# Keys times values straight from SBUF, values centred by their weight, and two projections side by side, in a three-stage transformer block

## The chip, the cores and the metric

The kernel runs on one core of a Trainium2 chip. The metric is the device time of one execution in microseconds (us); of several runs the median is given. PE is TensorE, DVE VectorE, ACT ScalarE, POOL GpSimd, SP the engine that only issues DMAs.

## The reference, cut to what matters

The input is `x` of 2 x 1024 tokens with 128 channels. Three stages follow each other:

```
x = x + 0.5 * ffn(layernorm(x))      # 8 experts, 128 -> 512 -> 128, the best 2 of 8 count
x = x + attn(layernorm(x))
x = x + 0.5 * ffn(layernorm(x))
```

Every expert is computed for every token and weighted by its gate. `attn` is a linear recurrence with 4 heads of 16 keys and 32 values:

```
r, k, v, g = four projections of token-shifted mixtures of x
w = tanh((x + delta * w_mu) @ A_w.T) @ B_w.T + b_w
S_t = exp(-exp(w_t)) * S_{t-1} + k_t v_t^T
o_t = r_t . (S_{t-1} + u * k_t v_t^T)
o = (o - mean(o)) / sqrt(var(o) + eps)        # over the 32 values of each head
attn = (o * gn_weight + gn_bias) * silu(g) @ W_o.T
```

`mean(o)` is linear in `v`, since `o` is.

## The kernel before, in words

**Layout.** The channels lie on the 128 partitions and 512 tokens are one tile, so there are 4 tiles (2 sequences, 2 halves each), and 8 blocks of feed-forward work (4 tiles before the attention, 4 after). The second halves take the recurrence's state over from the first.

**The slots.** The program is written out by hand as 256 slots `n`, one for each block, expert and quarter of the hidden width (`SLOTS`, `ALL`). In each slot PE computes one quarter up (`ffn_up`, L353, three matmuls L363, L364, L367 in fp32r, a split of fp32 into an upper and a lower part) and one quarter down, three slots late (`ffn_down`, L369). The quarter down is one fp32 matmul (L397), or, where `in_parts(n)` says so, three fp32r matmuls (L388, L390, L393), for which ACT writes `hid_hi` (L596) and DVE subtracts `hid_lo` (L798). ACT makes the relu of each quarter (L595, L598). After the four quarters of an expert DVE weights them with the gates (`combine`, L807) and POOL adds them to `x` (`add_y`, L954).

**The attention units.** Between the slots' feed-forward work stand the steps of the attention, one unit `i` for each tile (0 and 1 are the first halves, 2 and 3 the second). `UNIT` gives the slot where a unit begins, `step_of` its step `t` in slot `n`, and each engine's program has a function `attend(i, t)` that says what it does in that step. Every engine works strictly in the order written.

- `T_PR` (t = 12 to 14): projections. PE multiplies `u` by `A_w` (L502, bank A2, rows 0 to 63) and `W_r` (L503, bank A2, rows 64 to 127), by `W_k` (L506, all 128 rows of bank A1, the 64 outputs twice), and one slot on by `W_v` (L510); the last three through `proj`, whose matmul is L461. ACT takes the tanh (L652), copies `q` twice (L654, L655), `kk` (L657) and `v` (L660) out of PSUM. DVE forms `quk = q * bonus * kk` (L878).
- SP writes `v` to DRAM and reads it back as `vb`, one of 16 groups of rows at a time, each value row repeated over its keys (`values`, L289, `fetch`, L608). `vb` has 5 buffers.
- `T_SC` (t = 18 to 37): the recurrence, 16 steps `m` in 20 slots (`scan_at`). For each, ACT copies `vb` into one of three PSUM banks (`show`, L624), DVE multiplies that bank in place by `kk` (`keys_times_values`, L840; one step ahead), scans it along time with `dec` into a state buffer `S` (L856), and POOL multiplies the state by `q` (`read_state`, L995) after it has saved or seeded the carry (L992 or L1001, 1 column). There are 4 state buffers and 8 buffers `qs`.
- `REDUCE` (t = 25, 30, 35, 39): PE sums 4 of the `qs` over the keys (L469). `ROUTE` and other numbers place the router's small steps.
- `T_PO` (t = 40): PE centres `o` by a matmul (L523), ACT squares it (L672), DVE scales it (L894), and the variance, the output projection and the addition to `x` follow up to t = 48.

Of the kernel before, what the change touches and what calls it, by code (L numbers as in the profile page):

```python
# [5 lines left out]
ALU = mybir.AluOpType  # L6
# [146 lines left out]
def program(nc, xT_in, xtok_in, wexp_in, small_in, const_in, gate_dram, v_dram, out):  # L153
    with ExitStack() as ctx:
        def sb(name, shape, dt=F32):
            return ctx.enter_context(nc.sbuf_tensor(name, shape, dt))
# [87 lines left out]
        xa_zero, xa_prev, xm_r, z_p, z_r, mus, mterm, u_r = (sem(n) for n in ("xa_zero", "xa_prev", "xm_r", "z_p", "z_r", "mus", "mterm", "u_r"))  # L244
        pr, aw_r, q_r, k_r, quk_r, bet, bet_c, bv_r = (sem(n) for n in ("proj", "aw_r", "q_r", "k_r", "quk_r", "beta", "beta_c", "bv_r"))
        v_r, sg_t, sg_r, wb_r, e_r, dec_r = (sem(n) for n in ("v_r", "sg_t", "sg_r", "wb_r", "e_r", "dec_r"))
        vp, kv_r, st_r, qs_r, red, o_r, seed, s_zero = (sem(n) for n in ("vp", "kv_r", "st_r", "qs_r", "red", "o_r", "seed", "s_zero"))
        cen, sq_r, var_p, ysc_r, yoff_r, yo_r, yp, x_att = (sem(n) for n in ("cen", "sq_r", "var_p", "ysc_r", "yoff_r", "yo_r", "yp", "x_att"))

# [4 lines left out]
        def _(sp):  # L254
# [34 lines left out]
            def values(i):  # L289
                sp.wait_ge(v_r, i + 1)  # L290
                for d in range(VD):
                    sp.dma_start(v_dram[i].rearrange("(r d) n -> r d n", d=VD)[:, d, :], v[:, :]).then_inc(v_out[i], 16)
                sp.wait_ge(v_out[i], 16 * VD)
                for m in range(VS):
                    n = i * VG + m
                    if n >= VS:
                        sp.wait_ge(vp, n - VS + 1)
                    sp.dma_start(vb[:, n % VS, :], value_rows(v_dram[i], m)).then_inc(v_in[n % VS], 16)
# [51 lines left out]
        def _(pe):  # L350
# [95 lines left out]
            def mus_of(i, n):  # L446
                if n == 0:
                    pe.wait_ge(z_r, 2 * i + 1)
                if n == 2:
                    pe.wait_ge(z_r, 2 * i + 2)  # L450
                if n >= 3:
                    pe.wait_ge(mterm, 5 * i + n - 2)
                dst, c = A[MUS_BANK[n]][:, :], MIX[n]
                if c < 4:
                    mm(dst, w(W_X2, P, slice(32 * c, 32 * c + 32)), z0[32 * c:32 * c + 32, :],
                       start=True, stop=True).then_inc(mus, 1)
                else:
                    mm(dst, w(W_X2B, P, slice(0, 32)), z1, start=True, stop=True).then_inc(mus, 1)
# [14 lines left out]
            def attend(i, t):  # L473
# [25 lines left out]
                if t == T_PR:  # L499
                    pe.wait_ge(mterm, 5 * i + 4)  # L500
                    pe.wait_ge(u_r, 5 * i + 2)
                    mm(A[2][0:64, :], w(W_A, 64), u[:, 1, :], start=True, stop=True).then_inc(pr, 1)  # L502
                    mm(A[2][64:P, :], w(W_R, 64), u[:, 0, :], start=True, stop=True).then_inc(pr, 1)  # L503
                    pe.wait_ge(mterm, 5 * i + 5)
                    pe.wait_ge(u_r, 5 * i + 3)
                    proj(i, 1, W_K, 2)  # L506
                if t == T_PR + 1:
                    pe.wait_ge(q_r, i + 1)
                    pe.wait_ge(u_r, 5 * i + 4)
                    proj(i, 2, W_V, 3)  # L510
                    pe.wait_ge(aw_r, i + 1)
                    pe.wait_ge(quk_r, i + 1)
                    mm(A[0][:, :], w(W_B, P, slice(0, 64)), aw[0:64, :], start=True, stop=True).then_inc(wb_r, 1)
                    mm(A[1][:, :], const[64:P, C_BET:C_BET + P], quk[64:P, :], start=True, stop=True).then_inc(bet, 1)
# [4 lines left out]
                if t in REDUCE:  # L519
                    reduce(i, REDUCE.index(t))  # L520
                if t == T_PO:
                    pe.wait_ge(o_r, i + 1)
                    mm(A[0][:, :], const[:, C_CEN:C_CEN + P], o[:, :], start=True, stop=True).then_inc(cen, 1)  # L523
                if t == T_VAR:
# [35 lines left out]
        def _(act):  # L560
# [47 lines left out]
            def fetch(i, m):  # L608
                n = i * VG + m
                act.wait_ge(vp, n - VS + 1)  # L610
                act.dma_start(vb[:, n % VS, :], value_rows(v_dram[i], m)).then_inc(v_in[n % VS], 16)

            def show(i, m):
                n = i * VG + m
                if m == 0:
                    act.wait_ge(bet_c, i + 1)
                if m == 1:
                    act.wait_ge(bv_r, i + 1)
                if m == 2:
                    act.wait_ge(sg_r, i + 1)  # L620
                if m >= 3:
                    act.wait_ge(st_r, n - 2)
                act.wait_ge(v_in[n % VS], 16 * (n // VS + 1))
                act.activation(A[STATE_BANK[m % 3]][:, :], vb[:, n % VS, :], ACT.Copy).then_inc(vp, 1)  # L624

            def attend(i, t):
                h, b = home(i)
                if t == T_NRM:
                    normalise(LN_ATT[i], A[0])
                if scan_at(t + 1) == 0:  # L630
                    show(i, 0)
                if scan_at(t + 1) is not None and scan_at(t + 1) + 1 < VG:
                    m = scan_at(t + 1) + 1
                    show(i, m)
                    if m + VS - 1 < VG:
                        fetch(i, m + VS - 1)
                if t == T_CHN:
# [12 lines left out]
                if t == T_PR:  # L650
                    act.wait_ge(pr, 5 * i + 1)
                    act.activation(aw[0:64, :], A[2][0:64, :], ACT.Tanh).then_inc(aw_r, 1)  # L652
                    act.wait_ge(pr, 5 * i + 2)
                    act.activation(q[0:64, :], A[2][64:P, :], ACT.Copy)  # L654
                    act.activation(q[64:P, :], A[2][64:P, :], ACT.Copy).then_inc(q_r, 1)  # L655
                    act.wait_ge(pr, 5 * i + 3)
                    act.activation(kk[:, :], A[1][:, :], ACT.Copy).then_inc(k_r, 1)  # L657
                if t == T_PR + 1:
# [11 lines left out]
                if t == T_PO:  # L670
                    act.wait_ge(cen, i + 1)
                    act.activation(sq, A[0][:, :], ACT.Square).then_inc(sq_r, 1)  # L672
                    act.activation(y_off, sg[:, :], ACT.Identity, scale=w(W_GB, 1)).then_inc(yoff_r, 1)
# [23 lines left out]
        def _(dve):  # L697
# [138 lines left out]
            def keys_times_values(i, m):  # L836
                n = i * VG + m
                bank = A[STATE_BANK[m % 3]][:, :]
                dve.wait_ge(vp, n + 1)
                dve.tensor_tensor(bank, bank, kk[:, :], ALU.mult).then_inc(kv_r, 1)  # L840

            def scan(i, m):
                n, (h, b) = i * VG + m, home(i)
                bank = A[STATE_BANK[m % 3]][:, :]
                if m == 0:
                    keys_times_values(i, 0)
                if m + 1 < VG:
# [11 lines left out]
            def attend(i, t):  # L859
# [15 lines left out]
                if t == T_PR:  # L875
                    dve.wait_ge(q_r, i + 1)
                    dve.wait_ge(k_r, i + 1)
                    dve.scalar_tensor_tensor(out=quk[:, :], in0=q[:, :], scalar=w(W_U, 1), in1=kk[:, :],  # L878
                                             op0=ALU.mult, op1=ALU.mult).then_inc(quk_r, 1)
# [12 lines left out]
                if t == T_PO:  # L892
                    dve.wait_ge(sq_r, i + 1)
                    dve.scalar_tensor_tensor(out=y_sc, in0=A[0][:, :], scalar=w(W_GW, 1), in1=sg[:, :],  # L894
                                             op0=ALU.mult, op1=ALU.mult).then_inc(ysc_r, 1)
# [175 lines left out]
def lay_out(d):  # L1071
# [62 lines left out]
```

## Time and profile before

| | |
|---|---|
| median of 3 runs | 481.19 us (480.6 to 481.32) |
| the profiled execution's own time | 481.31 us |
| its span, first to last instruction | 479.5 us |
| PE busy | 466.3 us, 97% |
| DVE busy | 389.5 us, 81% |
| ACT busy | 341.2 us, 71% |
| POOL busy | 250.8 us, 52% |
| granted TensorE clock | 0.999 of full speed |
| chain that ended last | PE 61%, DVE 16%, issue 11%, POOL 5%, ACT 4%, DMA 2% |

Times in the views count from the first instruction. Matmuls are pipelined, so a PE row's length holds the time behind its neighbours too; the pace of PE is read from one start to the next.

### The profile page before, as it was taken

How to read it: one execution, taken by the hardware profiler on the slowest of the kernel's cores; microseconds unless marked ns; L12 is line 12 of the kernel's file. 1: busy time of each engine (PE TensorE's matmuls, PEld its weight loads, DVE VectorE, ACT ScalarE, POOL GpSimd, SP SyncE). 2: the span in 40 equal slices, each digit the busy share in tenths (PEclk: the TensorE clock that was granted, in tenths of full speed). 3: DMA queues.
4: the chain of work that ended last, by engine and by line, in shares of the span. 5: the costliest groups of instructions: out<-in, count | busy, mean ns of one | idle time of the engine just before them, and what ended most of it. 6: DMA issues, size and time to landing. Idle time of an engine off the chain costs nothing.

```text
span 479.5 us, 6566 instructions
## 1 busy us (share of the span) xinstructions
PE 466.3 (97%) x1977; PEld 295.9 (62%) x1977; DVE 389.5 (81%) x714; ACT 341.2 (71%) x585; POOL 250.8 (52%) x266
## 2 busy tenths in 40 slices
PE   7999989999999999999999999999999999999996
PEld 3667656565556647555654756566565555777785
DVE  3889987869977896997696799967679994786986
ACT  3787767687758768774867777656878665688784
POOL 1658463627885172886516268834617874321322
PEclk9999999999999999999999999999999999999999
DMA  8761040157310018630003554121056501004200
GB/s 260 226 243 42 1 130 27 46 162 234 131 45 0 3 45 223 194 110 1 2 1 131 154 179 153 44 67 44 0 157 204 173 24 39 2 0 132 68 1 22
DMA packets 21298, 44.60 MB, mean 93 GB/s; under 512 B 3856, under 2 KB 4240, under 8 KB 21264
## 3 DMA queue, kind: packets, MB, share of 16 engines
q1 hardware_dynamic: 14928, 32.66, 21.6%
q10 hardware_dynamic: 6336, 11.54, 8.1%
q8 instruction: 16, 0.26, 0.2%
q14 instruction: 18, 0.15, 0.1%
HBM read 40.91 MB, written 3.28 MB: 92 GB/s over the span
## 4 chain that ended last, share of the span: by engine, by line
PE 61%; DVE 16%; issue 11%; POOL 5%; ACT 4%; DMA 2%; POOLq 0%; SPq 0%; ACTq 0%; DVEq 0%
PE Y L397 13%; PE U L363 9%; PE U L367 8%; PE U L364 8%; DVE hid_lo L798 4%; PE Y L388 4%; PE Y L393 4%; PE Y L390 4%; PE A L469 3%; POOL xT L954 2%; DVE gy L807 2%; POOL qs L995 2%; PE A L461 1%; ACT hid_hi L596 1%; DMA G<-gate_dram 1%
## 5 line engine op out<-in xcount | busy, mean ns | idle before, releaser
L954 POOL TENSOR_TENSOR xT<-xT,gy 128x512 f32<-128x512 f32 x63 | 83.6, 1326 | 138.1 <-DVE gy L807 138.0
L363 PE MATMUL U<-xhi,w1lo 128*128 128x512 f32 x256 | 146.0, 570 | 1.9 <-ACT hid_hi L596 1.7
L798 DVE TENSOR_TENSOR hid_lo<-hid,hid_hi 128x512 fp32r<-128x512 f32 x140 | 117.1, 847 | 27.2 <-ACT hid_hi L596 25.8
L595 ACT ACTIVATE hid<-U,small 128x512 f32<-128x512 f32 x128 | 88.2, 689 | 41.9 <-PE U L367 37.6
L598 ACT ACTIVATE hid<-U,small 128x512 f32<-128x512 f32 x128 | 87.8, 689 | 41.6 <-PE U L367 38.9
L397 PE MATMUL Y<-hid,w 128*128 128x512 f32 x228 | 115.9, 589 | 0.0
L364 PE MATMUL U<-xhi,w1hi 128*128 128x512 f32 x256 | 100.8, 394 | 0.0
L367 PE MATMUL U<-xlo,w1hi 128*128 128x512 f32 x256 | 100.6, 393 | 0.0
L995 POOL TENSOR_TENSOR qs<-q,pool_a 128x512 f32<-128x512 f32 x64 | 79.9, 1248 | 16.0 <-DVE pool_a L856 16.0
L596 ACT ACTIVATE hid_hi<-U,small 128x512 fp32r<-128x512 f32 x128 | 87.6, 685 | 0.0
L363 PEld LDWEIGHTS U<-xhi,w1lo 128*128 128x128 f32 x256 | 48.1, 188 | 59.4 <-issue 33.3
L364 PEld LDWEIGHTS U<-xhi,w1hi 128*128 128x128 f32 x256 | 48.3, 189 | 27.5 <-issue 23.5
L367 PEld LDWEIGHTS U<-xlo,w1hi 128*128 128x128 f32 x256 | 48.0, 188 | 11.4 <-DVE xlo L734 0.4
L393 PE MATMUL Y<-hid_lo,w2hi 128*128 128x512 f32 (+1 forms) x134 | 52.5, 392 | 0.6 <-DVE hid_lo L798 0.6
L388 PE MATMUL Y<-hid_hi,w2lo 128*128 128x512 f32 (+1 forms) x134 | 52.1, 389 | 0.7 <-DVE hid_lo L798 0.7
L390 PE MATMUL Y<-hid_hi,w2hi 128*128 128x512 f32 (+1 forms) x134 | 52.0, 388 | 0.0
L624 ACT ACTIVATE A<-vb 128x512 f32<-128x512 f32 x64 | 38.1, 600 | 19.3 <-DVE pool_a L856 19.2
L807 DVE SCALAR_TENSOR_TENSOR gy<-Y,small,G 128x512 f32<-128x512 f32 x61 | 44.9, 736 | 5.1 <-DMA G<-gate_dram 3.6
L397 PEld LDWEIGHTS Y<-hid,w 128*128 128x128 f32 x228 | 42.8, 188 | 9.7
L840 DVE TENSOR_TENSOR A<-A,kk 128x512 f32<-128x512 f32 x64 | 43.1, 678 | 0.0
L856 DVE TENSOR_TENSOR_SCAN pool_a<-dec,carry,A 128x512 f32<-128x512 f32 x32 | 40.5, 1265 | 0.0
L856 DVE TENSOR_TENSOR_SCAN pool_a<-dec,A 128x512 f32<-128x512 f32 x32 | 38.5, 1204 | 0.0
(135 smaller groups left out, 526.6 us busy)
## 6 DMA issues: line engine op xcount, KB each, us to landing
G<-gate_dram SPq DMA_DIRECT2D x32, 512.0 KB, 4.5
vb<-v_dram ACTq DMA_DIRECT2D x44, 256.0 KB, 3.7
vb<-v_dram SPq DMA_DIRECT2D x20, 256.0 KB, 4.3
pool_a<-wexp_dram SPq DMA_DIRECT2D x8, 256.0 KB, 6.7
w<-wexp_dram SPq DMA_DIRECT2D x8, 256.0 KB, 6.6
v_dram<-v SPq DMA_DIRECT2D x8, 256.0 KB, 2.2
xnt<-xtok_dram SPq DMA_DIRECT2D x4, 256.0 KB, 4.9
xT<-xT_dram SPq DMA_DIRECT2D x4, 256.0 KB, 7.3
```

The costliest lines, as they stand in the source:

```text
L363: mm(dst, w1lo[:, e, f, :], xhi[:, k % NB, :], start=True, stop=False)
L364: mm(dst, w1hi[:, e, f, :], xhi[:, k % NB, :], start=False, stop=False)
L367: mm(dst, w1hi[:, e, f, :], xlo[:, k % NB, :], start=False, stop=True).then_inc(up, 1)
L393: last = mm(dst, w2hi[:, g % E, f, :], hid_lo[:, at, cut], start=False, stop=final)
L397: last = mm(dst, w2[:, g % E, f, :], hid[:, n % HS, cut], start=first, stop=final)
L595: act.activation(hid[:, n % HS, :], U[n % 2][:, :], ACT.Relu, bias=bias)
L596: act.activation(hid_hi[:, c % PS, :], U[n % 2][:, :], ACT.Relu, bias=bias).then_inc(h_f, 1)
L598: act.activation(hid[:, n % HS, :], U[n % 2][:, :], ACT.Relu, bias=bias).then_inc(h_f, 1)
L798: dve.tensor_tensor(hid_lo[:, c, :], hid[:, n % HS, :], hid_hi[:, c, :], ALU.subtract).then_inc(h_lo, 1)
L856: dve.tensor_tensor_scan(S[:, n % SS, 1:NT + 1], dec[:, :], bank, carry[:, b, m:m + 1] if h else 0.0, ALU.mult, ALU.add).then_inc(st_r, 1)
L954: pool.tensor_tensor(xT[:, h, b, :], xT[:, h, b, :], gy[:, g % 2, :], ALU.add).then_inc(acc, 1)
L995: pool.tensor_tensor(qs[:, n % QS, :], q[:, :], S[:, n % SS, 0:NT], ALU.mult).then_inc(qs_r, 1)
```

## The change

What it does, by parts:

1. `show` and its 64 ACT copies L624 are gone. DVE's `keys_times_values` reads `vb` in SBUF and `kk` in SBUF and writes the PSUM bank; it takes over the waits of `show`. The buffers of `vb` come free at `kv_r` (the product is made) in place of `vp` (the copy is made), and ACT's `fetch` of a row group stands at another slot.
2. The centring matmul L523 of each unit is gone. In unit 0's `T_Z` PE multiplies `W_v` by the centring matrix once (128 columns), ACT copies the product to `wv`, and the projection of `v` uses `wv`. `o` then comes out centred; the square and the scaling read it from SBUF.
3. `A_w`'s projection is cut into two halves of 256 tokens, one to rows 0 to 63 and one to rows 64 to 127 of bank A2; `W_r` and `W_k` go to rows 64 to 127 and 0 to 63 of bank A1, 64 outputs each. ACT makes two tanh of 64 x 256 and four copies of 64 x 512 (upper `q`, upper `kk`, lower `q`, lower `kk`) where it made one tanh, two copies of 64 rows and one of 128. `quk` is formed on the upper 64 partitions alone.

The core of the diff:

```
@@ sync, values
-                        sp.wait_ge(vp, n - VS + 1)
+                        sp.wait_ge(kv_r, n - VS + 1)
@@ tensor, attend
                 if t == T_Z:
                     pe.wait_ge(small_l, 16)
                     pe.wait_ge(xm_r, i + 1)
+                    if i == 0:
+                        pe.wait_ge(const_l, 16)
+                        mm(A[0][:, 0:P], w(W_V, P), const[:, C_CEN:C_CEN + P], start=True, stop=True).then_inc(cen, 1)
...
                 if t == T_PR:
                     pe.wait_ge(mterm, 5 * i + 4)
                     pe.wait_ge(u_r, 5 * i + 2)
-                    mm(A[2][0:64, :], w(W_A, 64), u[:, 1, :], start=True, stop=True).then_inc(pr, 1)
-                    mm(A[2][64:P, :], w(W_R, 64), u[:, 0, :], start=True, stop=True).then_inc(pr, 1)
+                    for c in range(2):
+                        last = mm(A[2][64 * c:64 * c + 64, 0:NT // 2], w(W_A, 64), u[:, 1, c * NT // 2:(c + 1) * NT // 2],
+                                  start=True, stop=True)
+                    last.then_inc(pr, 1)
                     pe.wait_ge(mterm, 5 * i + 5)
                     pe.wait_ge(u_r, 5 * i + 3)
-                    proj(i, 1, W_K, 2)
+                    mm(A[1][64:P, :], w(W_R, 64), u[:, 0, :], start=True, stop=True).then_inc(pr, 1)
+                    mm(A[1][0:64, :], w(W_K, 64), u[:, 2, :], start=True, stop=True).then_inc(pr, 1)
                 if t == T_PR + 1:
-                    pe.wait_ge(q_r, i + 1)
+                    pe.wait_ge(aw_r, i + 1)
                     pe.wait_ge(u_r, 5 * i + 4)
-                    proj(i, 2, W_V, 3)
-                    pe.wait_ge(aw_r, i + 1)
+                    mm(A[2][:, :], wv[:, :], u[:, 3, :], start=True, stop=True).then_inc(pr, 1)
+                    pe.wait_ge(qk_r, i + 1)
                     pe.wait_ge(quk_r, i + 1)
...
-                if t == T_PO:
-                    pe.wait_ge(o_r, i + 1)
-                    mm(A[0][:, :], const[:, C_CEN:C_CEN + P], o[:, :], start=True, stop=True).then_inc(cen, 1)
@@ scalar
-                act.activation(A[STATE_BANK[m % 3]][:, :], vb[:, n % VS, :], ACT.Copy).then_inc(vp, 1)
...
-                if scan_at(t + 1) == 0:
-                    show(i, 0)
-                if scan_at(t + 1) is not None and scan_at(t + 1) + 1 < VG:
-                    m = scan_at(t + 1) + 1
-                    show(i, m)
-                    if m + VS - 1 < VG:
-                        fetch(i, m + VS - 1)
+                if scan_at(t) is not None and VS <= scan_at(t) + VS - 1 < VG:
+                    fetch(i, scan_at(t) + VS - 1)
...
-                    act.wait_ge(cen, i + 1)
-                    act.activation(sq, A[0][:, :], ACT.Square).then_inc(sq_r, 1)
+                    act.wait_ge(o_r, i + 1)
+                    act.activation(sq, o[:, :], ACT.Square).then_inc(sq_r, 1)
@@ vector, keys_times_values
-                dve.wait_ge(vp, n + 1)
-                dve.tensor_tensor(bank, bank, kk[:, :], ALU.mult).then_inc(kv_r, 1)
+                if m == 0:
+                    dve.wait_ge(bet_c, i + 1)
+                if m == 1:
+                    dve.wait_ge(bv_r, i + 1)
+                if m == 2:
+                    dve.wait_ge(sg_r, i + 1)
+                if m >= 3:
+                    dve.wait_ge(st_r, n - 2)
+                dve.wait_ge(v_in[n % VS], 16 * (n // VS + 1))
+                dve.tensor_tensor(bank, vb[:, n % VS, :], kk[:, :], ALU.mult).then_inc(kv_r, 1)
```

How the instructions stand at the two places that matter. On ACT, at the start of unit 0's recurrence (`A<-vb` is the copy of a value row group into a PSUM bank, the DMA fetches the group that is used some steps on), before:

```order
L624 ACTIVATE A<-vb 128x512 [waits v_in0,beta_c]
L624 ACTIVATE A<-vb 128x512 [waits v_in1,bv_r]
L611 DMA vb<-v_dram 128x1x512 [waits vp]
L598 ACTIVATE hid<-U,small 128x512 [waits down,up]
L624 ACTIVATE A<-vb 128x512 [waits v_in2,sg_r]
L611 DMA vb<-v_dram 128x1x512 [waits vp]
L595 ACTIVATE hid<-U,small 128x512 [waits down,up]
```

And the same place of the changed kernel:

```order
L616 DMA vb<-v_dram 128x1x512 [waits kv_r]
L603 ACTIVATE hid<-U,small 128x512 [waits down,up]
L616 DMA vb<-v_dram 128x1x512 [waits kv_r]
L603 ACTIVATE hid<-U,small 128x512 [waits down,up]
L616 DMA vb<-v_dram 128x1x512 [waits kv_r]
```

Only relus and DMA issues are left there; the first DMA stands two slots later than before.

On DVE, the same stretch (`A<-A,kk` is the product made in the PSUM bank, `pool_a<-dec,A` the scan, `hid_lo` the feed-forward's split, `gy` its weighting), before:

```order
L807 SCALAR_TENSOR_TENSOR gy<-Y,small,G 128x512 [waits acc,g_in0,down]
L840 TENSOR_TENSOR A<-A,kk 128x512 [waits vp] x2
L856 SCALAR_TENSOR_TENSOR pool_a<-dec,A 128x512 [waits kv_r,dec_r]
L840 TENSOR_TENSOR A<-A,kk 128x512 [waits vp]
L856 SCALAR_TENSOR_TENSOR pool_a<-dec,A 128x512 [waits kv_r]
L798 TENSOR_TENSOR hid_lo<-hid,hid_hi 128x512 [waits h_f]
L840 TENSOR_TENSOR A<-A,kk 128x512 [waits vp]
```

And in the changed kernel, where the product by chance stands in line 840 too:

```order
L799 SCALAR_TENSOR_TENSOR gy<-Y,small,G 128x512 [waits acc,g_in0,down]
L840 TENSOR_TENSOR A<-vb,kk 128x512 [waits v_in0,beta_c,qk_r]
L840 TENSOR_TENSOR A<-vb,kk 128x512 [waits v_in1,bv_r]
L857 SCALAR_TENSOR_TENSOR pool_a<-dec,A 128x512 [waits kv_r,dec_r]
L840 TENSOR_TENSOR A<-vb,kk 128x512 [waits v_in2,sg_r]
L857 SCALAR_TENSOR_TENSOR pool_a<-dec,A 128x512 [waits kv_r]
L790 TENSOR_TENSOR hid_lo<-hid,hid_hi 128x512 [waits h_f]
```

DVE's order is the same; what the product reads and waits for is another.

## Rows read from the trace of the kernel before

**Rows 1.** Busy times, unit 0's recurrence; x counts instructions, then clock, DMA share, GB/s
```profile
core 0: us, PE busy (x) PEld busy (x) DVE busy (x) ACT busy (x) POOL busy (x), PEclk, DMA share, GB/s
105.40:143.15 37.75, 37.75 (x150) 22.04 (x148) 34.84 (x43) 27.00 (x45) 30.60 (x39) 1.00 0.49 148
```

**Rows 2.** Groups by line: busy us, mean ns | idle before
```profile
L624 ACT ACTIVATE A<-vb 128x512 f32<-128x512 f32 x64 | 38.1, 600 | 19.3 <-DVE pool_a L856 19.2
L840 DVE TENSOR_TENSOR A<-A,kk 128x512 f32<-128x512 f32 x64 | 43.1, 678 | 0.0
```

**Rows 3.** Timeline of DVE in unit 2's recurrence: start us, length us, engine, line
```profile
302.27 1.27 DVE L856 TENSOR_TENSOR_SCAN pool_a<-dec,carry,A 128x512 f32<-128x512 f32 x1
303.46 0.93 DVE L798 TENSOR_TENSOR hid_lo<-hid,hid_hi 128x512 fp32r<-128x512 f32 x1
304.31 0.69 DVE L840 TENSOR_TENSOR A<-A,kk 128x512 f32<-128x512 f32 x1
304.91 1.27 DVE L856 TENSOR_TENSOR_SCAN pool_a<-dec,carry,A 128x512 f32<-128x512 f32 x1
```

**Rows 4.** Timeline of POOL in the same stretch
```profile
302.42 0.19 POOL L1001 COPY pool_a<-carry 128x1 f32<-128x1 f32 x1
302.56 1.28 POOL L954 TENSOR_TENSOR xT<-xT,gy 128x512 f32<-128x512 f32 x1
303.80 1.74 POOL L995 TENSOR_TENSOR qs<-q,pool_a 128x512 f32<-128x512 f32 x1
```

**Rows 5.** Timeline of DVE and POOL in unit 1's projections
```profile
177.89 0.75 DVE L878 SCALAR_TENSOR_TENSOR quk<-q,small,kk 128x512 f32<-128x512 f32 x1
...
177.96 1.80 POOL L954 TENSOR_TENSOR xT<-xT,gy 128x512 f32<-128x512 f32 x1 [0.70 <-DVE gy L807]
```

**Rows 6.** Line L995: ns min/median/max, first and last start, forms
```profile
L995 POOL TENSOR_TENSOR qs<-q,pool_a x64: 1087/1277/1746, 108.9 to 395.9; 128x512 f32<-128x512 f32 x64
```

**Rows 7.** First products (DVE) and last reads (POOL) of units 0 and 2, timeline
```profile
106.27 1.29 DVE L840 TENSOR_TENSOR A<-A,kk 128x512 f32<-128x512 f32 x2
...
140.00 1.30 POOL L995 TENSOR_TENSOR qs<-q,pool_a 128x512 f32<-128x512 f32 x1
...
276.00 1.29 DVE L840 TENSOR_TENSOR A<-A,kk 128x512 f32<-128x512 f32 x2
...
310.32 1.72 POOL L995 TENSOR_TENSOR qs<-q,pool_a 128x512 f32<-128x512 f32 x1
```

**Rows 8.** Last reduces of units 0 and 2 on PE, timeline
```profile
142.15 1.06 PE L469 MATMUL A<-qs,const 128*32 128x512 f32 x8
...
312.09 1.07 PE L469 MATMUL A<-qs,const 128*32 128x512 f32 x8 [0.70 <-POOL qs L995]
```

**Rows 9.** Two plain slots of PE, then the slot with the centring matmul, timeline
```profile
129.02 0.39 PE L364 MATMUL U<-xhi,w1hi 128*128 128x512 f32 x1
...
130.57 0.40 PE L364 MATMUL U<-xhi,w1hi 128*128 128x512 f32 x1
...
143.48 0.39 PE L364 MATMUL U<-xhi,w1hi 128*128 128x512 f32 x1
...
144.81 1.02 PE L523 MATMUL A<-o,const 128*128 128x512 f32 x2
145.26 0.79 PE L363 MATMUL U<-xhi,w1lo 128*128 128x512 f32 x1
145.90 0.40 PE L364 MATMUL U<-xhi,w1hi 128*128 128x512 f32 x1
```

**Rows 10.** PE in unit 0's projections, timeline
```profile
93.32 0.64 PE L502 MATMUL A<-pool_a,small 128*64 128x512 f32 x1
93.33 0.64 PE L503 MATMUL A<-pool_a,small 128*64 128x512 f32 x1
93.80 0.59 PE L502 MATMUL A<-pool_a,small 128*64 128x512 f32 x1
```

**Rows 11.** Waits of PE's weight loads: us in total, times, longest us
```profile
PEld A L461 <- DVE pool_a L873: 0.8, 1, 0.8
```

**Rows 12.** The page's DMA issues: count, KB each, median us to landing
```profile
vb<-v_dram ACTq DMA_DIRECT2D x44, 256.0 KB, 3.7
```

More of the change, by code:

```diff
@@ L169, in program @@
         const = sb("const", [P, C_ALL])
+        wv = sb("wv", [P, P])
         turn = sb("turn", [P, NB, P])
@@ L244, in program @@
         xa_zero, xa_prev, xm_r, z_p, z_r, mus, mterm, u_r = (sem(n) for n in ("xa_zero", "xa_prev", "xm_r", "z_p", "z_r", "mus", "mterm", "u_r"))
-        pr, aw_r, q_r, k_r, quk_r, bet, bet_c, bv_r = (sem(n) for n in ("proj", "aw_r", "q_r", "k_r", "quk_r", "beta", "beta_c", "bv_r"))
+        pr, aw_r, q_r, k_r, qk_r, quk_r, bet, bet_c, bv_r = (sem(n) for n in ("proj", "aw_r", "q_r", "k_r", "qk_r", "quk_r", "beta", "beta_c", "bv_r"))
         v_r, sg_t, sg_r, wb_r, e_r, dec_r = (sem(n) for n in ("v_r", "sg_t", "sg_r", "wb_r", "e_r", "dec_r"))
-        vp, kv_r, st_r, qs_r, red, o_r, seed, s_zero = (sem(n) for n in ("vp", "kv_r", "st_r", "qs_r", "red", "o_r", "seed", "s_zero"))
-        cen, sq_r, var_p, ysc_r, yoff_r, yo_r, yp, x_att = (sem(n) for n in ("cen", "sq_r", "var_p", "ysc_r", "yoff_r", "yo_r", "yp", "x_att"))
+        kv_r, st_r, qs_r, red, o_r, seed, s_zero = (sem(n) for n in ("kv_r", "st_r", "qs_r", "red", "o_r", "seed", "s_zero"))
+        cen, wv_r, sq_r, var_p, ysc_r, yoff_r, yo_r, yp, x_att = (sem(n) for n in ("cen", "wv_r", "sq_r", "var_p", "ysc_r", "yoff_r", "yo_r", "yp", "x_att"))
         block = ctx.enter_context(nc.Block())
@@ L447, in mus_of @@
                 if n == 0:
+                    pe.wait_ge(wv_r, 1)
                     pe.wait_ge(z_r, 2 * i + 1)
@@ L609, in fetch @@
                 n = i * VG + m
-                act.wait_ge(vp, n - VS + 1)
+                act.wait_ge(kv_r, n - VS + 1)
                 act.dma_start(vb[:, n % VS, :], value_rows(v_dram[i], m)).then_inc(v_in[n % VS], 16)
[L613 to L623, printed above, removed]
-                act.activation(A[STATE_BANK[m % 3]][:, :], vb[:, n % VS, :], ACT.Copy).then_inc(vp, 1)
             def attend(i, t):
@@ L642, in attend @@
                 if t == T_Z:
+                    if i == 0:
+                        act.wait_ge(cen, 1)
+                        act.activation(wv[:, :], A[0][:, 0:P], ACT.Copy).then_inc(wv_r, 1)
                     act.wait_ge(z_p, 2 * i + 1)
@@ L651, in attend @@
                     act.wait_ge(pr, 5 * i + 1)
[L652 to L655, printed above, removed]
+                    for c in range(2):
+                        last = act.activation(aw[0:64, c * NT // 2:(c + 1) * NT // 2], A[2][64 * c:64 * c + 64, 0:NT // 2], ACT.Tanh)
+                    last.then_inc(aw_r, 1)
                     act.wait_ge(pr, 5 * i + 3)
-                    act.activation(kk[:, :], A[1][:, :], ACT.Copy).then_inc(k_r, 1)
+                    act.activation(q[64:P, :], A[1][64:P, :], ACT.Copy).then_inc(q_r, 1)
+                    act.activation(kk[64:P, :], A[1][0:64, :], ACT.Copy).then_inc(k_r, 1)
+                    act.activation(q[0:64, :], A[1][64:P, :], ACT.Copy)
+                    act.activation(kk[0:64, :], A[1][0:64, :], ACT.Copy).then_inc(qk_r, 1)
                 if t == T_PR + 1:
@@ L845, in scan @@
                 if m == 0:
+                    dve.wait_ge(qk_r, i + 1)
                     keys_times_values(i, 0)
@@ L877, in attend @@
                     dve.wait_ge(k_r, i + 1)
-                    dve.scalar_tensor_tensor(out=quk[:, :], in0=q[:, :], scalar=w(W_U, 1), in1=kk[:, :],
+                    dve.scalar_tensor_tensor(out=quk[64:P, :], in0=q[64:P, :], scalar=w(W_U, 1, slice(64, P)), in1=kk[64:P, :],
                                              op0=ALU.mult, op1=ALU.mult).then_inc(quk_r, 1)
@@ L892, in attend @@
                 if t == T_PO:
-                    dve.wait_ge(sq_r, i + 1)
-                    dve.scalar_tensor_tensor(out=y_sc, in0=A[0][:, :], scalar=w(W_GW, 1), in1=sg[:, :],
+                    dve.wait_ge(o_r, i + 1)
+                    dve.scalar_tensor_tensor(out=y_sc, in0=o[:, :], scalar=w(W_GW, 1), in1=sg[:, :],
                                              op0=ALU.mult, op1=ALU.mult).then_inc(ysc_r, 1)
@@ L1090, in lay_out @@
     s[0:64, W_B:W_B + P] = np.tile(g["B_w"].T, (1, NS))
-    for at, name in ((W_V, "W_v"), (W_G, "W_g")):
-        s[:, at:at + P] = g[name].reshape(NH, NS, VG, P).transpose(3, 2, 1, 0).reshape(P, P)
+    s[:, W_V:W_V + P] = g["W_v"].reshape(NH, NS, VG, P).transpose(2, 1, 0, 3).reshape(P, P)
+    s[:, W_G:W_G + P] = g["W_g"].reshape(NH, NS, VG, P).transpose(3, 2, 1, 0).reshape(P, P)
     s[:, W_O:W_O + P] = g["W_o"].reshape(P, NH, NS, VG).transpose(3, 2, 1, 0).reshape(P, P)
```

## The prediction

> **What bounds the kernel now.** I read the busy table of the recurrence stages first, then the groups by line, then DVE's and POOL's timelines side by side, and last PE's pace from one start to the next. In unit 0's recurrence PE is busy 37.75 of 37.75 us at a granted clock of 1.00 (2.4 GHz) [rows 1]: PE is the bound, and an engine that is relieved beside it gives nothing by itself. But DVE is nearly full there too (34.84 us, with POOL at 30.60), so there is little room for DVE and POOL to grow longer before PE waits for them. Where that shows is the last reduce of each unit, which needs the last `qs` of POOL. In unit 0 that read ends at 140.00 + 1.30 = 141.30 [rows 7] and PE comes to the reduce at 142.15 [rows 8]: 0.85 us of slack. In unit 2 it ends at 312.04 and PE starts at 312.09 after an idle 0.70: no slack. Units 0 and 2 stand for their pairs (0, 1 and 2, 3) in all that follows.
>
> **Part 1, ACT's copies go: nothing directly.** They are 64 x 600 ns = 38.1 us, and half of their waiting (19.2 us) is ACT waiting for DVE's scan to free a bank [rows 2]. They stand beside a PE that never waits in this stage [rows 1], so they cost nothing now and give nothing back. The product itself keeps its length when it is alone: 0.69 us, 0.60 from its start to the next start [rows 3].
>
> **Part 1, what the product now reads.** The rows show two kinds of DVE instruction beside POOL. L840 before (one input in PSUM, one in SBUF) takes 0.69 us while POOL's L995 is at work, 678 ns in the mean of 64 and with no idle before any [rows 2, 3, 4]. L798 has both inputs in SBUF: it is issued at 303.46 while L954 runs (302.56 to 303.84), ends at 304.39, 0.55 after L954 has ended, and L995, issued at 303.80, ends at 305.54, 1.15 after L798's end [rows 3, 4]. The two never overlap: each waits for the other's whole instruction, DVE going first when both wait. L878 (`q`, `kk`, two SBUF inputs) does the same to L954: it runs its 0.75, and L954, issued 0.07 later, takes 1.80 instead of 1.28 [rows 4, 5]. The changed product has two SBUF inputs and, unlike these, writes PSUM; no row shows that mix. Its price per product lies between nothing (it behaves as L840) and a full exclusion (as L798, L878). I take the full one: L878 and L798 differ from L840 in the inputs, and the locked side cannot be the output, since the scan L856 (one SBUF tensor, one PSUM bank) writes SBUF and takes the same 1.27 us beside L954 and beside L995 [rows 3, 4].
>
> The Trainium skill ("SBUF — State Buffer", section "Who interferes with whom") says that a DVE instruction with two SBUF inputs contends with a GpSimd instruction that reads SBUF, because its second input comes through a shared read interface; it names no condition on the output. By that rule the sum is the one below; without it, it would be the first rival's. The trace agrees as far as outputs in SBUF go.
>
> The price of exclusion, per recurrence, as a queue of instructions that cannot overlap:
> - 16 steps, each one copy of a carry (0.14 from start to start), one product (0.60) and one read of the state (1.15 behind a DVE instruction) [rows 3, 4]: 16 x 1.89 = 30.2 us.
> - 5 additions L954 (one in 4 of 20 slots), 1.24 each [rows 4]: 6.2 us. 5 splits L798 at 0.60: 3.0 us.
> - Before the first read, one scan runs with nothing of POOL beside it, 1.19 [rows 3]: 1.2 us.
>
> That is 40.6 us from the first product to the end of the last read. Before it is 141.30 - 106.27 = 35.0 us in unit 0 and 312.04 - 276.00 = 36.0 in unit 2 [rows 7]. So units 0 and 1 end their reads 5.6 us later, 2 and 3 4.6 us later. Off goes the slack of 0.85 in the first pair [rows 7, 8], none in the second: 2 x 4.75 + 2 x 4.6 = **+18.7 us** of waiting by PE, at the reduces and in the slots before them. Of the queue behind the waiting instructions: DVE's splits and weightings and ACT's relus are pulled back with it, but they wait for the same thing and are not added again. With qs at its shortest, 1.09 [rows 6], the queue is 39.6 and the sum 4 less; with 1.28, it is 42.7 and the sum 8 more.
>
> **Part 1, the fetches** move past two slots of ACT's queue. One lands in 3.7 us [rows 12]; there are still three steps of the recurrence between a fetch and its use, over 3 x 1.8 us at DVE's pace (0.60 + 1.19 [rows 3]), longer with the exclusion. Nothing, and if the cover is gone, up to 1 us a unit.
>
> **Part 2, centring.** From L364 to L364 a plain slot is 130.57 - 129.02 = 1.55 us; the slot with L523 is 145.90 - 143.48 = 2.42 [rows 9]. The matmul costs PE 0.87, four times: **-3.5 us**, in slots where PE works without a pause. The one product of weights has 128 columns: a quarter, +0.2. ACT's copy of it stands ahead of a tanh that PE waits for in unit 0: +0.3 at most, taken in full.
>
> **Part 3, the projections.** L502 and L503 run at the same time in two column halves (starts 93.32 and 93.33, second pass at 93.80 [rows 10]); a pass of 512 columns is 0.48. Before, two pairs of passes for `A_w` beside `W_r` and two for `W_k`, 4 x 0.48. After, `A_w`'s halves side by side take two passes of 256, 2 x 0.24, and `W_r` beside `W_k` 2 x 0.48: -0.48 a unit. In one unit PE waits 0.8 us before `W_k` for a term of DVE [rows 11], which now holds `W_r` too, so I count three: **-1.4 us**. ACT has two instructions more here (two short tanh for one, four half copies for three), so `v` leaves later by less than one copy's 0.6 [rows 2]; it goes to DRAM and back over several slots before the first product, and the exclusion's wait does not depend on it. Nothing. If this cover is gone, the first product is late by up to 0.6 a unit.
>
> **The sum.** 18.7 - 3.5 + 0.5 - 1.4 = +14.3 us against the profiled execution's own 481.31 us: 495.6 us. That execution lies 0.12 above the median of 481.19, which leaves the number where it is.
>
> **The rivals.**
> - *No exclusion, faster.* If only instructions that also write SBUF are shut out, DVE keeps its pace (it is gapless before and after) and PE keeps its savings: 481.3 - 3.5 + 0.5 - 1.4 = **476.9 us**. For it: no row shows an output in PSUM. Against it: L856 writes SBUF and is not shut out. The point from which it decides: whether the product beside L995 takes 0.69 or more. Chance 0.11.
> - *Half the price.* If the conflicts fall partly into DVE's and POOL's own pauses, each product costs POOL about half: the queue is 35.0 (36.0) + half of 5.6 (4.6), so 2 x (2.8 - 0.85) + 2 x 2.3 = 8.5 us, and the time is 481.3 + 8.5 - 4.4 = **485.4 us**. Against it: POOL has to wait for the scan in each step, so its pauses cannot be filled ahead of time. Chance 0.10.
> - *POOL goes first.* If at the end of each scan POOL gets in ahead of DVE, nothing overlaps the scan: 0.60 + 1.19 + 1.29 = 3.1 us a step, 49 us and the additions, above 58 in all, 4 x 23 us more: over 560 us. DVE's next instruction starts before the recorded end of a scan (303.46 against 303.54 [rows 3]), POOL only behind a semaphore, so I give a mild mixture of this, 505 to 515 us, 0.06.
> - *The change does not do what it says:* DVE's order is unchanged and ACT's copies are gone from the program, so no chance of its own.
>
> **How the numbers follow.** A measurement of this kernel tells 0.2%, about 1 us, from no change. Forecast (full exclusion, 490 to 505): 0.73. Slower cases together are forecast, half price and POOL first: 0.89, of which 0.02 could be eaten up to within 0.2%. So faster 0.11, same 0.02, slower 0.87. The forecast's own range is 491 to 504 (the two lengths of qs). The range reaches down to the half price and up over the uncovered costs of parts 1 and 3 (4 x 1 us): 485 to 506, which leaves out the fast rival and the worst mixture.
>
> **What would show it.** Right: the product's mean length well above 0.69 us, lengths of L995 near 1.7 to 1.9 in most of its 64, DVE and POOL never at once in product and read, PE idle of some 4 to 5 us around the last reduce of each unit, waits "weight load of the reduce for POOL's qs" grown from a few us to near 19, and the centring gone with slots of 1.55 there. Wrong: a product of 0.69 beside L995 (first rival), or waits on `vb`'s DMA ahead of the product (the fetches' cover), or a granted clock below 1.00 where PE pauses.

## The result, and the profile after

The changed kernel takes **496.60 us** (median of 4 runs, 494.38 to 496.98) against 481.25 us (median of 4, 480.60 to 481.32) before: a ratio of 1.0312, 95% interval 1.0281 to 1.0344. The medians are 15.35 us apart; the forecast was 495.6 (485 to 506).

The busy table of the four recurrence stages, from the first of 22 slots to the slot behind the last reduce, answers to [rows 1]:

```profile
core 0: us, PE busy (x) PEld busy (x) DVE busy (x) ACT busy (x) POOL busy (x), PEclk, DMA share, GB/s
105.15:146.54 41.39, 39.73 (x149) 22.96 (x148) 38.09 (x43) 18.83 (x29) 36.81 (x39) 0.96 0.49 140
189.09:230.44 41.35, 38.51 (x147) 21.49 (x145) 38.36 (x43) 19.40 (x30) 35.65 (x38) 1.00 0.45 130
278.32:323.11 44.79, 39.88 (x148) 21.47 (x146) 43.32 (x47) 19.41 (x30) 35.92 (x38) 0.97 0.31 100
369.89:414.48 44.59, 39.71 (x148) 21.48 (x146) 40.88 (x43) 18.25 (x28) 37.00 (x38) 0.97 0.39 119
```

Unit 0's stage is 3.6 us longer than its 37.75 before; over all four the stages grew by 17.4 us (their lengths before were 37.75, 38.24, 39.46 and 39.30), more than the kernel lost. ACT has nearly a third less work (18.83 us in place of 27.00 in unit 0), but PE, which never paused in unit 0, is idle for 1.7 us there and for 2.8 to 4.9 us in the others (44.79 - 39.88 in unit 2), and the granted clock is no longer 1.00 in three of the four.

The groups by line, answering to [rows 2]; columns as there:

```profile
L996 POOL TENSOR_TENSOR qs<-q,pool_a 128x512 f32<-128x512 f32 x64 | 88.3, 1380 | 12.4 <-DVE pool_a L857 12.4
L840 DVE TENSOR_TENSOR A<-vb,kk 128x512 f32<-128x512 f32 x64 | 59.2, 929 | 0.4 <-DMA vb<-v_dram 0.4
L471 PE MATMUL A<-qs,const 128*32 128x512 f32 x128 | 18.8, 662 | 11.9 <-POOL qs L996 11.9
L993 POOL COPY carry<-pool_a 128x1 f32<-128x1 f32 x32 | 14.5, 453 | 7.6 <-DVE pool_a L857 6.0
```

The same product takes 929 ns in place of 678, POOL's carry copy 453 in place of 286, and PE stands idle 11.9 us ahead of its reduces, where it was 0.7. The 0.4 us on the DMA of `vb` are one wait, for the second value group of unit 0, which is none of the fetches that part 1 moved. It is found only in kernels with part 3 (0.4 and 1.3 us in the two traces of experiment 1's kernel, 1.3 in that of part 3 alone), and not before the change or with part 1 alone.

DVE's and POOL's timelines in unit 2, answering to [rows 3, 4], show how it happens:

```profile
300.21 1.34 DVE L840 TENSOR_TENSOR A<-vb,kk 128x512 f32<-128x512 f32 x1
301.47 1.27 DVE L857 TENSOR_TENSOR_SCAN pool_a<-dec,carry,A 128x512 f32<-128x512 f32 x1
302.66 0.72 DVE L840 TENSOR_TENSOR A<-vb,kk 128x512 f32<-128x512 f32 x1
303.29 1.27 DVE L857 TENSOR_TENSOR_SCAN pool_a<-dec,carry,A 128x512 f32<-128x512 f32 x1
304.49 0.66 DVE L790 TENSOR_TENSOR hid_lo<-hid,hid_hi 128x512 fp32r<-128x512 f32 x1
305.07 0.69 DVE L840 TENSOR_TENSOR A<-vb,kk 128x512 f32<-128x512 f32 x1
```

```profile
300.94 0.65 POOL L1002 COPY pool_a<-carry 128x1 f32<-128x1 f32 x1
301.55 1.28 POOL L955 TENSOR_TENSOR xT<-xT,gy 128x512 f32<-128x512 f32 x1
302.82 1.70 POOL L996 TENSOR_TENSOR qs<-q,pool_a 128x512 f32<-128x512 f32 x1
304.46 0.73 POOL L1002 COPY pool_a<-carry 128x1 f32<-128x1 f32 x1
305.15 1.55 POOL L996 TENSOR_TENSOR qs<-q,pool_a 128x512 f32<-128x512 f32 x1
```

L955 ends at 302.83, the product that has waited since 302.66 runs to 303.38, and only then does L996, issued at 302.82, get going, to end at 304.52. A copy of one column, issued at 300.94 beside a product, takes 0.65 where a free one takes 0.19. The scans keep their 1.27 beside all of it. The median product is 0.69 us and the longest 1.79: a product that need not wait loses nothing and POOL does.

In all of these the DVE instruction had been issued first. Six microseconds earlier POOL's was, and it went first:

```profile
296.30 0.66 DVE L790 TENSOR_TENSOR hid_lo<-hid,hid_hi 128x512 fp32r<-128x512 f32 x1
296.88 1.58 DVE L840 TENSOR_TENSOR A<-vb,kk 128x512 f32<-128x512 f32 x1
...
296.45 1.46 POOL L996 TENSOR_TENSOR qs<-q,pool_a 128x512 f32<-128x512 f32 x1 [0.19 <-DVE pool_a L857]
```

The read L996 is issued while the split L790 runs (to 296.96) and ends at 297.91; the product behind the split, issued 0.43 after the read, waits for it and ends at 298.46, 0.55 later. So what these rows show is that the instruction goes first that was issued first, and not that DVE has precedence.

First product and last read of unit 2, answering to [rows 7], and PE behind the read, answering to [rows 8]:

```profile
280.68 0.69 DVE L840 TENSOR_TENSOR A<-vb,kk 128x512 f32<-128x512 f32 x1
...
319.48 1.71 POOL L996 TENSOR_TENSOR qs<-q,pool_a 128x512 f32<-128x512 f32 x1
...
321.25 1.93 PE L471 MATMUL A<-qs,const 128*32 128x512 f32 x8 [3.56 <-POOL qs L996]
323.11 0.80 PE L364 MATMUL U<-xhi,w1lo 128*128 128x512 f32 x1
323.70 0.63 PE L365 MATMUL U<-xhi,w1hi 128*128 128x512 f32 x1
324.13 0.63 PE L368 MATMUL U<-xlo,w1hi 128*128 128x512 f32 x1
...
326.69 0.50 PE L368 MATMUL U<-xlo,w1hi 128*128 128x512 f32 x1
327.03 0.40 PE L389 MATMUL Y<-hid_hi,w2lo 128*128 128x512 f32 x1
327.26 0.40 PE L391 MATMUL Y<-hid_hi,w2hi 128*128 128x512 f32 x1
```

From 280.68 to 321.19 are 40.5 us, 4.5 more than before. PE has idled 3.56 us when it starts the reduce, and behind the pause its matmuls start 0.43 us apart, not 0.23, until 326.7: the granted clock is 0.50 there, its lower level (1.2 GHz).

Where the centring matmul stood, the slots are plain again, as [rows 9] would have them without it (148.44 - 146.88 = 1.56):

```profile
146.88 0.39 PE L365 MATMUL U<-xhi,w1hi 128*128 128x512 f32 x1
...
148.44 0.40 PE L365 MATMUL U<-xhi,w1hi 128*128 128x512 f32 x1
```

### The profile page after: what moved, and what is told of

It is laid out like the page before. It is cut to its first block, busy times and chain, and to the rows that moved or that the text cites. A ratio compares the mean times of both kernels' runs of the same rounds, so it can differ in the third digit from the quotient of the medians.

```text
span 494.6 us, 6519 instructions
## 1 busy us (share of the span) xinstructions
PE 468.4 (95%) x1979; PEld 297.0 (60%) x1979; DVE 404.8 (82%) x714; ACT 310.1 (63%) x530; POOL 278.1 (56%) x266
## 4 chain that ended last, share of the span: by engine, by line
PE 40%; issue 20%; DVE 15%; POOL 15%; ACT 5%; DMA 4%; POOLq 0%; SPq 0%; DVEq 0%; ACTq 0%
PE U L364 6%; PE Y L398 6%; POOL xT L955 5%; PE U L365 5%; PE U L368 5%; POOL qs L996 5%; DVE hid_lo L790 4%; PE Y L394 3%; PE Y L389 3%; PE Y L391 3%; POOL pool_a L1002 2%; DMA vb<-v_dram 2%; DVE gy L799 2%; PE A L471 2%; ACT hid_hi L601 1%
## 5 line engine op out<-in xcount | busy, mean ns | idle before, releaser
L955 POOL TENSOR_TENSOR xT<-xT,gy 128x512 f32<-128x512 f32 x63 | 88.2, 1400 | 136.6 <-DVE gy L799 136.5
L790 DVE TENSOR_TENSOR hid_lo<-hid,hid_hi 128x512 fp32r<-128x512 f32 x140 | 116.0, 839 | 28.5 <-ACT hid_hi L601 26.9
L996 POOL TENSOR_TENSOR qs<-q,pool_a 128x512 f32<-128x512 f32 x64 | 88.3, 1380 | 12.4 <-DVE pool_a L857 12.4
L840 DVE TENSOR_TENSOR A<-vb,kk 128x512 f32<-128x512 f32 x64 | 59.2, 929 | 0.4 <-DMA vb<-v_dram 0.4
L857 DVE TENSOR_TENSOR_SCAN pool_a<-dec,carry,A 128x512 f32<-128x512 f32 x32 | 40.6, 1268 | 0.0
L960 POOL TENSOR_TENSOR rstd<-std,half 128x4 f32<-128x4 f32 x12 | 14.9, 1245 | 34.8 <-DVE std L716 34.8
```

The source lines that it names most:

```text
L790: dve.tensor_tensor(hid_lo[:, c, :], hid[:, n % HS, :], hid_hi[:, c, :], ALU.subtract).then_inc(h_lo, 1)
L857: dve.tensor_tensor_scan(S[:, n % SS, 1:NT + 1], dec[:, :], bank, carry[:, b, m:m + 1] if h else 0.0, ALU.mult, ALU.add).then_inc(st_r, 1)
L955: pool.tensor_tensor(xT[:, h, b, :], xT[:, h, b, :], gy[:, g % 2, :], ALU.add).then_inc(acc, 1)
L996: pool.tensor_tensor(qs[:, n % QS, :], q[:, :], S[:, n % SS, 0:NT], ALU.mult).then_inc(qs_r, 1)
```

## The experiments

Two questions were open: whether it is the product's second SBUF input that costs (theory A) or something else that came with it (B, parts 2 and 3; C, the moved waits and fetches), and what each other part is worth alone. The kernel before ran beside them at 481.02 to 481.28 us.

**1. Part 1 undone** (`e1_psum_values`): the changed kernel with `show` back.

```
-dve.tensor_tensor(bank, vb[:, n % VS, :], kk[:, :], ALU.mult)
+act.activation(bank, vb[:, n % VS, :], ACT.Copy)        # show(i, m), with its old waits and place
+dve.tensor_tensor(bank, bank, kk[:, :], ALU.mult)
```

> The changed kernel with part 1 undone: ACT copies the value rows to PSUM again, the centring by the weight and the projections side by side stay. Theory A (the product's two SBUF inputs exclude POOL's reads): all of the loss goes with the copy, and what parts 2 and 3 save stands alone: 481.3 - 3.5 + 0.5 - 1.0 = 477.3 us, 476.3 to 478.3; products back at 0.68 us. Theory B (the loss comes from parts 2 and 3, such as the wait for all four half copies ahead of the beta matmul): still over 490 us.

Measured: 476.13 us, ratio 0.9902 (0.9889 to 0.9915), 0.2 below the range expected. The product is back at a mean of 684 ns. All of the loss goes with part 1; what is left is better than the kernel before. A second measurement of it, for experiment 8:

> The kernel of e1_psum_values once more, beside e8_late_upper_q on the same chip, since the two lie within 0.5 us by either expectation: 476.1 us, 475.8 to 476.5.

Measured: 476.59 us, ratio 0.9911 (0.9897 to 0.9924), 0.1 above the range expected.

**2. Part 1 alone** (`e2_part1_alone`): that part of the diff on the kernel before.

> The kernel before with part 1 alone: the product reads the value rows and the keys from SBUF, no ACT copies; centring and projections as before. Theory A: 496.6 + 4.0 = 500.6 us, 499 to 502, last read of each unit 3.5 to 4.6 us later after its first product than before, PE waiting over 4 us ahead of the last reduces of units 2 and 3. Theory B: 481 to 484.

Measured: 500.81 us, ratio 1.0409 (1.0385 to 1.0432). Part 1 costs 19.8 us by itself and 20.5 on top of parts 2 and 3 (496.60 - 476.13), so the parts hardly touch each other.

**3. One SBUF input** (`e3_one_sbuf_input`): the run that tells the second input from everything else. The product leaves out the keys and takes what the bank held before in their place.

```
-dve.tensor_tensor(bank, vb[:, n % VS, :], kk[:, :], ALU.mult)
+dve.tensor_tensor(bank, bank, vb[:, n % VS, :], ALU.mult)
```

> The changed kernel, but the product takes the old content of its PSUM bank and the value rows (one input in PSUM, one in SBUF) instead of the value rows and the keys (both in SBUF); it leaves the keys out of the product. Order, waits, DMAs and the freed ACT are those of the changed kernel. Theory A (the second SBUF input excludes POOL): products at 0.68 us, L996 back to a mean near 1.25, 477 us (476 to 478.5). Theory C (what costs is the chain without the ACT copy: buffers of the value rows freed later, the copy's waits now in DVE's queue, later fetches): products' waits stay and the time stays over 490 us.

Measured: 476.33 us, ratio 0.9904 (0.9891 to 0.9917). Its groups by line:

```profile
L996 POOL TENSOR_TENSOR qs<-q,pool_a 128x512 f32<-128x512 f32 x64 | 79.2, 1237 | 16.1 <-DVE pool_a L857 16.1
L840 DVE TENSOR_TENSOR A<-A,vb 128x512 f32<-128x512 f32 x64 | 43.5, 686 | 0.0
L471 PE MATMUL A<-qs,const 128*32 128x512 f32 x128 | 17.1, 605 | 1.2 <-POOL qs L996 1.2
```

Same order, same DMAs, same waits in DVE's queue, and the product is back at 686 ns, POOL's read at 1237, PE's idle time at 1.2 us. Nor is it one of the two SBUF tensors by itself: the product with `kk` and a bank takes 684 ns (experiment 1), that with `vb` and a bank 686. Theory C is out: DVE has no idle time before its product (0.0), so the moved waits and fetches cost nothing that can be measured. The run says one thing more. It has no ACT copies and no exclusion, which is all that part 1 could hope for, and it is not faster than the kernel of experiment 1 with its 64 copies (476.13 and 476.59). So ACT's 38 us were worth nothing, unless a gain from them was eaten up by a cost of the moved waits of which the trace has no sign.

**4. Every second product** (`e10_every_second`): for even `m` the product is that of `show`, for odd `m` that of the change.

> The changed kernel with every second product (even m) on a PSUM bank that ACT fills, the others on two SBUF inputs: half the exclusion. If the price goes by the number of products: reads end 1.8 us later (units 0, 1) and 2.3 us later (units 2, 3) than without, less 0.7 us of slack in the first two, 2 x 1.1 + 2 x 2.3 = 6.8 us on 476.3, and hardly a low clock, since no pause reaches 3 us: 483.1 us, 482 to 484.5. If half the conflicts find room in DVE's and POOL's own pauses, as the second rival of the prediction had it: 477 to 480.5. If the alternation of two forms costs more than either: over 485.

Measured: 488.35 us (486.71 to 489.90), ratio 1.0162 (1.0140 to 1.0183), 5 us above the 483.1 expected. By group:

```profile
L863 DVE TENSOR_TENSOR A<-vb,kk 128x512 f32<-128x512 f32 x32 | 33.6, 1050 | 0.0
L852 DVE TENSOR_TENSOR A<-A,kk 128x512 f32<-128x512 f32 x32 | 21.6, 676 | 0.1
```

In one kernel, with the same scans around them, the two forms take 1050 and 676 ns. Half the products cost more than half the price: 12.2 us against 20.5. The rival "half the price" is refuted in its mechanism too: with half the conflicts, each left costs DVE more (1050 ns against 929) and not less, so they do not vanish into DVE's and POOL's pauses. Why it is more than half is only argued: ACT's copies now wait for a scan that the exclusion has made late (34.4 us of that wait ahead of 32 copies in its trace, 19.2 ahead of 64 in [rows 2]), and relus stand behind them.

**5. Centring alone** (`e4_centring_alone`), part 2 on the kernel before.

> The kernel before with part 2 alone (values centred by the weight, no centring matmul). By my sum four matmuls of 0.87 us leave PE, one of a quarter comes: 481.3 - 3.5 + 0.5 = 478.3 us, 477.5 to 479. If the matmul stood in time that PE had to wait through anyway: 481.

Measured: 477.99 us, ratio 0.9930 (0.9917 to 0.9943).

**6. Projections alone** (`e5_projections_alone`), part 3 on the kernel before.

> The kernel before with part 3 alone. My sum gave -0.48 us in three of four units, 481.1 - 1.4 = 479.7. The trace of the changed kernel shows PE waiting for ACT's last half copy ahead of the beta matmul in units 1 and 2, so: 481.1 - 1.0 = 480.1 us, 479.3 to 480.6.

Measured: 479.88 us, ratio 0.9979 (0.9970 to 0.9988). Waits of PE's weight loads in it:

```profile
PEld A L516 <- ACT kk L662: 4.8, 4, 1.9
```

L516 is the matmul by `W_b` that now waits for the last half copy. PE itself idles ahead of it in two of four units, 0.56 us in unit 1 and 1.07 in unit 2 (0.17 and 0.44 before), and what the two column halves save is given back there.

**7. The clock** (`e6_keep_clock`).

```
+if n == 3 and i >= 2:
+    pe.wait_ge(st_r, i * VG + 14)
+    for _ in range(3):
+        mm(A[2][:, :], const[:, C_CEN:C_CEN + P], sg[:, :], start=True, stop=True)
 pe.wait_ge(qs_r, i * VG + 4 * n + 4)
```

> The changed kernel with three matmuls more (128x512, fp32, their result not used) on PE ahead of the last reduce of units 2 and 3, where it idles over 4 us; they wait for the scan before the last but one, so that they fall into the pause. Theory D (the pauses bring the granted clock to 1.2 GHz for 3.4 to 6.8 us behind them, and that costs time): no low clock after these two reduces, slots 163 and 164 back to their length, 496.6 - 2.5 = 494.1 us, 493.4 to 495. Theory E (the low clock falls where PE would wait anyway): 496.6, 496 to 497.5.

Measured: 492.40 us, ratio 1.0241 (1.0225 to 1.0257): 4.2 us off the changed kernel by giving PE more work, and 4.0 if each is taken against the runs of before beside it. The runs of the two do not overlap (492.19 to 493.36, 494.38 to 496.98). PE in unit 2, at the place shown above:

```profile
318.09 2.74 PE L469 MATMUL A<-sg,const 128*128 128x512 f32 x6
321.83 1.07 PE L475 MATMUL A<-qs,const 128*32 128x512 f32 x8 [1.01 <-POOL qs L1000]
322.83 0.50 PE L364 MATMUL U<-xhi,w1lo 128*128 128x512 f32 x1
323.17 0.39 PE L365 MATMUL U<-xhi,w1hi 128*128 128x512 f32 x1
323.40 0.40 PE L368 MATMUL U<-xlo,w1hi 128*128 128x512 f32 x1
```

The pause is 1.01 us instead of 3.56, the reduce takes 1.07 instead of 1.93, and matmuls start 0.23 us apart at once. Lined up slot by slot, the changed kernel's trace loses 2.7 us to this one in unit 2 and 1.4 in unit 3. Theory E is out; D was right with the price set too low.

**8. Where the lower half copies stand** (`e7_late_low_copies`, `e8_late_upper_q`), on the kernel of experiment 1. The label of the second is a slip: it moves the lower half of `q`.

```
 # ACT, T_PR: two tanh, upper q, upper kk
-act.activation(q[0:64, :], A[1][64:P, :], ACT.Copy)
-act.activation(kk[0:64, :], A[1][0:64, :], ACT.Copy).then_inc(qk_r, 1)
 # e7: both copies from SBUF, behind the tanh of the gate (T_PR + 2)
+act.activation(q[0:64, :], q[64:P, :], ACT.Copy)
+act.activation(kk[0:64, :], kk[64:P, :], ACT.Copy).then_inc(qk_r, 1)
 # e8: lower kk stays where it was, lower q alone moves, to T_PR + 4
+act.activation(q[0:64, :], q[64:P, :], ACT.Copy).then_inc(qk_r, 1)
```

> The kernel of e1_psum_values (values shown in PSUM, centring by the weight, projections side by side), but ACT makes the two lower half copies of q and kk from SBUF and behind the tanh of the gate, so that the beta matmul waits for quk alone. PE then waits less in units 1 and 2 (0.6 and 1.1 us of idle there, quk is ready 0.45 us ahead of the last copy): 476.1 - 0.9 = 475.2 us, 474.7 to 475.8. If something else is late there: 476.1.

Measured: 479.17 us, ratio 0.9958 (0.9946 to 0.9971), 4 us above what was expected and 3 above the kernel of experiment 1. ACT's and PE's weight loads at the new place of the copies, in unit 0:

```profile
101.69 0.63 ACT L679 ACTIVATE q<-q 64x512 f32<-64x512 f32 x1
102.23 0.61 ACT L680 ACTIVATE kk<-kk 64x512 f32<-64x512 f32 x1
102.86 0.69 ACT L599 ACTIVATE hid<-U,small 128x512 f32<-128x512 f32 x1
103.45 0.68 ACT L600 ACTIVATE hid_hi<-U,small 128x512 fp32r<-128x512 f32 x1
...
104.18 0.19 PEld L364 LDWEIGHTS U<-xhi,w1lo 128*128 128x128 f32 x1 [0.86 <-ACT hid_hi L600]
```

The relu L599 starts at 102.86; in the kernel of experiment 1, with no copies ahead of it, it starts at 102.05. PE has only feed-forward work there and runs into it. At their old place the copies lie beside the matmuls of the projections, where no relu is due. So one copy was moved, to a slot with a single relu:

> The kernel of e1_psum_values, with one instead of two copies moved: ACT takes lower kk from PSUM right behind upper kk, and lower q from SBUF four slots later (step 16 of the unit), where the relu is single. The beta matmul then waits for quk (0.75 us) and one copy (0.6) side by side instead of two copies (1.2), which e7_late_low_copies showed to be worth 0.1 us in unit 1 and 0.4 in unit 2; what that one lost was PE waiting for relus behind the moved copies in slots 53, 95, 137 and 181 (0.4 to 0.7 us each), and here only one copy stands in a slot with a single relu. 476.1 - 0.5 = 475.6 us, 475.2 to 476. If one copy of 0.6 us there is too much as well: 476.5 to 478.

Measured: **476.00 us**, ratio 0.9895 (0.9881 to 0.9908), 0.6 us below the kernel of experiment 1 on the same chip. It computes what the reference does and has the lowest median of all: parts 2 and 3 without part 1. That the move itself gains is not shown: the lead is 0.6 us over the second measurement of experiment 1's kernel (476.46 to 477.34 against 475.79 to 476.38) and 0.1 over the first (476.02 to 476.85).

## Why the prediction was right

**Part 1, the mechanism.** Right, and shown by experiments 1, 3 and 4: a DVE instruction with a second SBUF input shuts POOL's reads out while it runs, and the other way round, also where the output is in PSUM. That was the point no row of before could settle. The Trainium skill ("SBUF — State Buffer", "Who interferes with whom") names the inputs alone; the trace agrees, with 929 or 1050 ns for two SBUF inputs and 676 to 686 for one, on the same bank.

**Part 1, the size.** The +18.7 us came out as +19.8 to +20.5, but its inside was different. The queue of 40.6 us measured 38.65 and 38.86 in units 0 and 1, and 40.51 and 40.68 in units 2 and 3. So the reads end 3.6, 3.7, 4.5 and 4.6 us later behind the first product than before; less the slack (0.85, and 0.7 in unit 1) that is some 14.9 us of PE's waiting, not 18.7. The term that was too large is the read at 1.15: I let each one stand behind a DVE instruction, but 7 and 6 of the 16 in units 0 and 1 run in under 1.15 in all, and only 2 of 16 in units 2 and 3, where the queue fits. What made up for it was not in the sum at all: the clock, 4.2 us by experiment 7, which took the pauses of units 2 and 3 away. I had named it only as a sign that would speak against me, and it came. Two errors of about 4 us cancelled: that the time lies within 1 us of the forecast is luck, while the direction and the cause are not.

14.9 and 4.2 leave about 1 us of the 19.8 to 20.5. Most of it is the clock again, in the middle of unit 0, behind a pause ahead of an earlier reduce:

```profile
127.89 1.06 PE L471 MATMUL A<-qs,const 128*32 128x512 f32 x8 [1.22 <-POOL qs L996]
...
129.00:132.40 3.40, 3.40 (x6) 2.05 (x7) 3.40 (x4) 1.27 (x2) 3.40 (x4) 0.51 0.37 100
```

PE comes out of it so late that its last reduce starts at 145.54, 0.87 us behind the last read's end; with part 1 alone, where the clock stayed at 1.00 there, it starts 0.05 behind. That is 0.8 us. PE's weight loads also wait 6.9 us for DVE's splits, where it was 1.8, and which part of that lies beside the waits counted above was not separated.

**ACT's copies at nothing.** Right (experiment 3). Their wait was misread, though nothing hangs on it: the 19.2 us for DVE's scan are nearly all of the 19.3 that they waited [rows 2], and not half. **The fetches at nothing.** Right. The one wait on `vb` (0.4 us) came with part 3, whose later `v` I had put at nothing.

**Part 2.** -3.5 + 0.5 = -3.0 forecast, 477.99 - 481.04 = -3.05 measured.

**Part 3.** -1.4 forecast, -1.2 measured alone. The step was right, its cover was not: I counted the second wait on ACT's copies as hidden, and in units 1 and 2 PE waits 0.4 and 0.6 us longer than before, for the last of them and for the `quk` that DVE forms from the upper ones. Together parts 2 and 3 give 4.7 to 4.9 (4.4 forecast).

**The rivals.** "No exclusion" would have been 476.9, and experiment 3 shows what it stood for: 476.33. "Half the price" and "POOL goes first" did not happen. My reading that DVE goes first when both wait does not hold: in [rows 3, 4] L798 had been issued 0.34 us before L995, and where POOL's read was issued first it went first (L996 at 296.45, above). The queue's sum does not hang on that order.

**The signs.** The waits of the reduce for `qs` grew to 22.4 us in PE's weight loads (19 expected), the product's mean to 929 ns, and POOL's long reads are there, though in a part of the 64 only: 15 take 1.6 us or more, their mean is 1380 ns, and the rest of the price is DVE's. PE's idle time of 4 to 5 us came in units 2 and 3, and 1.7 and 2.8 in the first two.

## What to carry to other kernels

Before a copy to PSUM is taken away, see what it shields: a DVE instruction with two SBUF inputs and a GpSimd instruction that reads SBUF take turns, so where both engines are busy in one loop, one operand in PSUM is worth an idle engine's copy. Add up a loop's shared work (here 40.6 us by the sum against 35 to 36 us of room), not each engine's own. And where a change makes PE, the bound engine here, wait for microseconds in one piece, the clock behind the pause can cost most of that again (2.7 us behind 3.56 in unit 2, 1.4 in unit 3).

## What the runs showed that I had not expected

A pause of PE of 3.56 us cost more than itself. The granted clock (the third number from the end) from 321.0 to 326.5 in the changed kernel:

```profile
321.00:326.50 5.50, 5.25 (x16) 2.92 (x17) 3.35 (x5) 1.70 (x3) 1.42 (x2) 0.50 0.03 8
```

It does not fall behind every pause: in that trace it is 1.00 behind the pause of 2.37 us in unit 1, and in the kernel with half the exclusion behind pauses of 1.67, 2.46 and 2.47. Nor does it fall in every run: experiment 7's kernel, which is the same in unit 0, has 1.00 from 129.0 to 132.4 in its trace and the changed kernel 0.51, and behind unit 1's pause it is the other way round (0.55 from 230.0 to 233.4, against 1.00). Over whole runs: of the changed kernel's four runs three had a mean clock of 0.986 and took 496.44 to 496.98 us, one had 0.993 and took 494.38. Of the kernel with half the exclusion, the profiled run had 1.000 and took 486.71, and another 0.992 and 489.90. So part of the scatter of such a kernel is its clock, and two kernels whose pauses differ have to be compared over several runs each. What decides whether a pause brings the clock down was not tested.
